# Rounded passes for the late blocks of the value product, a deferred sum, a third turn of scatter tables and shorter scatters

## The reference

```python
q = _rope(einsum('bim,ghmd->bghid', x, w_aq)); k = _rope(einsum('bim,gmd->bgid', x, w_ak))
v = einsum('bim,gmd->bgid', x, w_av)                     # G = 4 groups, H = 4 heads, D = 128
s = einsum('bghid,bgjd->bghij', q * D**-0.25, k * D**-0.25) - 1e30 * (i < j)
o = einsum('bghij,bgjd->bghid', softmax(s), v)           # the value product
x = _layernorm(x + einsum('bghid,ghdm->bim', o, w_ao))   # the out-projection and its sum
# experts: grouped top-6 of 64 by sigmoid scores; of an expert's tokens those with a place below CAP = 48 count
y = segment_sum(topk_w * (silu(buf @ w_gate) * (buf @ w_up)) @ w_down)
out = _layernorm(x + y + (silu(x @ ws_gate) * (x @ ws_up)) @ ws_down)
```

## Time and profile before

| | us |
|---|---|
| median of 3 runs | 1127.45 (1126.43 to 1128.49) |
| the profiled execution | 1126.55, its span 1124.7 |
| PE busy | 1017.0 (90%) |
| DVE busy | 562.6 (50%) |
| ACT busy | 518.7 (46%) |
| POOL busy | 363.4 (32%) |
| mean granted clock of PE | 0.96 |

### The profile page before, as it was taken

How to read it: one execution, slowest core, us unless ns; L and a number is a source line. 1 busy time by engine, 2 the same in 40 slices (tenths; PEclk the granted TensorE clock), 3 DMA queues, 4 the chain that set the end, 5 groups by cost and what they waited for, 6 DMA issues and landing times.

```text
span 1124.7 us, 16829 instructions
## 1 busy us (share of the span) xinstructions
PE 1017.0 (90%) x5312; PEld 731.9 (65%) x5312; DVE 562.6 (50%) x1533; ACT 518.7 (46%) x1147; POOL 363.4 (32%) x402
## 2 busy tenths in 40 slices
PE   6999998789999999999998899999999999657825
PEld 4888887566667776767666666777776676434512
DVE  5766765365554454443425675454535444323306
ACT  3333334454564556454543555464645645133312
POOL 6666665123322212103033313313021121035641
PEclk9999999799999999999999999999999999868868
DMA  7455233533321111111113323333211033968558
GB/s 230 163 180 183 105 117 108 163 91 106 95 63 62 53 56 49 38 43 51 34 44 98 101 80 95 112 104 100 65 39 52 26 92 91 245 178 175 80 100 315
DMA packets 99462, 117.57 MB, mean 105 GB/s; under 512 B 16065, under 2 KB 69173, under 8 KB 99376
## 3 DMA queue, kind: packets, MB, share of 16 engines
q1 hardware_dynamic: 76752, 87.65, 25.3%
q10 hardware_dynamic: 13408, 22.09, 6.5%
q0 software_dynamic: 9216, 6.76, 4.0%
HBM read 76.48 MB, written 53.35 MB: 115 GB/s over the span
## 4 chain that ended last, share of the span: by engine, by line
PE 75%; DMA 9%; DVE 6%; issue 4%; ACT 3%; SPq 2%; POOL 1%; ACTq 0%; POOLq 0%; DVEq 0%
PE o_ps L986 21%; PE s_ps L963 16%; PE ring L973 11%; PE ring L994 10%; DMA sums<-erow,goal_u 6%; PE s_ps L934 6%; PE ring L934 5%; PE s_ps L941 1%; SPq L657 1%; PE s_ps L966 1%; DVE neg_max L1150 1%; ACT probs L820 1%; DMA fsum<-sums 1%; PE o_ps L934 1%; PE ring L941 1%
## 5 line engine op out<-in xcount | busy, mean ns | idle before, releaser
L986 PE MATMUL o_ps<-pt,v 128*128 128x512 f32 x576 | 297.2, 598 | 3.9 <-DVE ot L1165 3.8
L828 ACT ACTIVATE pt<-ring 128x512 f32<-128x512 f32 x288 | 170.9, 594 | 252.1 <-PE ring L973 251.8
L963 PE MATMUL s_ps<-kt,qt_hi 128*128 128x512 f32 (+3 forms) x768 | 261.3, 422 | 3.5 <-issue 1.9
L1150 DVE TENSOR_REDUCE neg_max<-s_ps 128x1 f32<-128x128 f32 (+7 forms) x256 | 191.8, 753 | 135.8 <-PE s_ps L966 135.2
L820 ACT ACTIVATE probs<-s_ps,neg_max 128x128 f32<-128x128 f32 (+7 forms) x256 | 189.3, 740 | 110.2 <-DVE neg_max L1150 102.4
L718 POOL TENSOR_TENSOR qt_lo<-q_raw,qt_hi 128x512 fp32r<-128x512 f32 x64 | 81.2, 1270 | 474.1 <-ACT qt_hi L758 474.1
L963 PEld LDWEIGHTS s_ps<-kt,qt_hi 128*128 128x128 f32 x768 | 139.4, 194 | 79.4 <-issue 61.2
L973 PE MATMUL ring<-ident,probs 128*128 128x128 f32 x1152 | 176.2, 276 | 11.4 <-ACT probs L820 11.3
L973 PEld LDWEIGHTS ring<-ident,probs 128*128 128x128 f32 x1152 | 129.3, 142 | 56.8 <-issue 56.8
L963 PE MATMUL s_ps<-kt,qt_lo 128*128 128x512 f32 (+3 forms) x384 | 134.2, 350 | 0.0
L729 POOL DMA_INDIRECT slot_rows<-row,slot_u x96 | 94.5, 984 | 66.5 <-DVE slot_u L1267 39.7
(11 more groups left out here) (182 smaller groups left out, 1283.7 us busy)
## 6 DMA issues: line engine op xcount, KB each, us to landing
q_rows<-q_out SPq DMA_DIRECT2D x64, 256.0 KB, 2.0
q_raw<-q_rows ACTq DMA_DIRECT2D x64, 256.0 KB, 2.7
inv_row<-inverses SPq DMA_DIRECT2D x64, 256.0 KB, 3.3
fsum<-sums SPq DMA_DIRECT2D x32, 256.0 KB, 6.9
sums<-blank SPq DMA_DIRECT2D x16, 384.0 KB, 2.8
wexp<-in_L_ffn_w_gate_dram SPq DMA_DIRECT2D x32, 192.0 KB, 3.9
wexp<-in_L_ffn_w_up_dram SPq DMA_DIRECT2D x32, 192.0 KB, 4.2
wexp<-in_L_ffn_w_down_dram SPq DMA_DIRECT2D x32, 192.0 KB, 5.0
```

The costliest lines, as they stand in the source:

```text
L828: reader(act.activation(pt[:, n % PTB, :], bank(s), ACT.Copy), s)
L963: pe.matmul(s_ps[:, n % 2, c + a:c + e], q[qp], k[kp][:, a:e], start=(qp == kp == 0), stop=(qp == 1 and not last))
L986: pe.matmul(o_ps[:, :], v_sb[i // NT][:, g, j, :], pt[:, n % PTB, :], start=(j == 0), stop=(j == blocks(u) - 1)).then_inc(pv_done, 1)
L1150: dve.tensor_reduce(neg_max[:, n % 8:n % 8 + 1], s_ps[:, n % 2, score_cols(n)], AX_X, ALU.max, negate=True).then_inc(max_ready, 1)
```

## The change

- For key blocks 3 to 7 (VF = 3) the value product runs as three rounded passes: V and the transposed probabilities are split into a rounded high part (ACT, with the copy it made anyway) and a low part, DVE's subtraction out of PSUM. It is DVE's subtraction that lets the ring bank go. Blocks 0 to 2 stay as they were.
- There is room for one sequence's late V halves only. Those of the second sequence go to memory (v_rows) in the projection and come back group by group as the last tile of the first sequence is done with a group ("vsplit": ACT the high part, POOL the low).
- DVE's and POOL's part of "outproj" becomes a step "yadd", placed at heads (6, 6, 7, 7) where outproj is at (6, 7, 6, 6); norm and all behind it in the later tiles are placed one head later.
- TURNS 3 instead of 2 (6 tables, EB 6), so half as many bytes again to clear and to read back; the scatter-adds take 112 rows (64 + CAP) instead of 128.
- XB, the buffers of x, 2 instead of 3. The value tiles take other places, so that homes come free at other times.

```diff
-EB = 4
-TURNS = 2
+EB = 6
+TURNS = 3
+USED = HALF + CAP
-XB = 3
+XB = 2
+VF = 3
+VS = NT - VF
...
     (("outproj",), -1, (6, 7, 6, 6)),
-    (("norm",), -1, (7, 7, 7, 7)),
-    (("x1t",), -1, (9, 9, 8, 8)),
-    (("rtr",), -1, (11, 11, 9, 9)),
-    (("shared",), -1, (11, 11, 9, 9)),
-    (("pick", 0), -1, (12, 12, 10, 10)),
+    (("yadd",), -1, (6, 6, 7, 7)),
+    (("norm",), -1, (7, 7, 8, 8)),
+    (("x1t",), -1, (9, 9, 9, 9)),
+    (("rtr",), -1, (11, 11, 10, 10)),
+    (("shared",), -1, (11, 11, 10, 10)),
+    (("pick", 0), -1, (12, 12, 11, 11)),
...
             seq.append(("omul", u))
+            if u // G == NT - 1:
+                seq.append(("vsplit", u % G))
...
-        v_sb = [sb("v0", [P, G, NT, D], F32, att)]
+        v_sb = [sb("v0", [P, G, VF, D], F32, att)]
...
+        v = sb("v", [P, G, 2, VS, D], F32R, att)
...
+        pt_hi = sb("pt_hi", [P, PTB, HD], F32R, att)
+        pt_lo = sb("pt_lo", [P, PTB, HD], F32R, att)
...
-                    load_x(s[1] + 2)
+                    load_x(s[1] - 1 + XB)
...
+                if s[0] == "proj" and s[2] == "V" and s[1] >= NT + VF:
+                    j = s[1] - NT - VF
+                    read(sp, s)
+                    sp.dma_start(v_rows[j * P:(j + 1) * P, :], v_out[:, :]).then_inc(v_stored, 16)
+                if s == ("omul", G * (NT - 2)):
+                    sp.wait_ge(v_stored, 16 * VS)
+                    load_v(0)
+                if s[0] == "vsplit" and s[1] + 1 < G:
+                    sp.wait_ge(v_later, s[1] + 1)
+                    load_v(s[1] + 1)
...
-                    load_homes(kt[0], v_sb[0], kt[1], *[v_sb[1][:, 0, :, :]] * (G - 1))
+                    load_homes(kt[0], v_sb[0], kt[1], *[v[:, 0, :, :, :]] * (G - 1))
...
-                if s[0] == "outproj":
+                if s[0] == "vsplit":
+                    g = s[1]
+                    pool.wait_ge(v_later_hi, g + 1)
+                    pool.tensor_tensor(v[:, g, 1, :, :], v_raw[:, :, :], v[:, g, 0, :, :].bitcast(F32), ALU.subtract
+                                       ).then_inc(v_later, 1)
+                if s[0] == "yadd":
                     pool.wait_ge(var_ready, s[1] + 1)
...
-                    sums[:, :], bass.IndirectOffsetOnAxis(ap=goal_u[:, n:n + 1], axis=0),
-                    erow[:, n % EB, :], None, bounds_check=TABLES * TABLE - 1, oob_is_err=True, compute_op=ALU.add
+                    sums[:, :], bass.IndirectOffsetOnAxis(ap=goal_u[0:USED, n:n + 1], axis=0),
+                    erow[0:USED, n % EB, :], None, bounds_check=TABLES * TABLE - 1, oob_is_err=True, compute_op=ALU.add
...
-                    reader(act.activation(pt[:, n % PTB, :], bank(s), ACT.Copy), s)
+                    if s[2] < VF:
+                        reader(act.activation(pt[:, n % PTB, :], bank(s), ACT.Copy), s)
+                    else:
+                        split(pt_hi[:, n % PTB, :], bank(s)).then_inc(p_hi_ready, 1)
...
-                    pe.matmul(o_ps[:, :], v_sb[i // NT][:, g, j, :], pt[:, n % PTB, :],
-                              start=(j == 0), stop=(j == blocks(u) - 1)).then_inc(pv_done, 1)
+                    first, last = j == 0, j == blocks(u) - 1
+                    if j < VF:
+                        ins = pe.matmul(o_ps[:, :], v_sb[i // NT][:, g, j, :], pt[:, n % PTB, :], start=first, stop=last)
+                    else:
+                        for vp, pp in PASSES:
+                            ins = pe.matmul(o_ps[:, :], v[:, g, vp, j - VF, :], (pt_hi, pt_lo)[pp][:, n % PTB, :],
+                                            start=False, stop=(last and vp == 1))
+                    ins.then_inc(pv_done, 1)
...
+                if kind == "ptrans" and s[2] >= VF:
+                    n = PT_AT[s[1:]]
+                    dve.wait_ge(p_hi_ready, PS_AT[s[1:]] + 1)
+                    reader(low(pt_lo[:, n % PTB, :], bank(s), pt_hi[:, n % PTB, :]), s)
...
-                if kind == "outproj":
-                    i = s[1]
+                if kind == "yadd":
+                    i, s = s[1], ("outproj", s[1])
                     dve.wait_ge(attn_ready, i + 1)
```

More of the change, by code:

```diff
@@ L81 @@
     (("outproj",), -1, (6, 7, 6, 6)),
[L82 to L93 removed]
+    (("yadd",), -1, (6, 6, 7, 7)),
[4 more added lines that the diff above has]
+    (("pick", 0), -1, (12, 12, 11, 11)),
+    (("ht",), -1, (13, 13, 12, 12)),
+    (("pick", 1), -1, (13, 13, 12, 13)),
+    (("sd",), -1, (15, 15, 13, 13)),
+    (("pick", 2), -1, (14, 14, 13, 13)),
+    (("pick", 3), -1, (14, 14, 14, 14)),
+    (("pick", 4), -1, (14, 14, 14, 14)),
+    (("pick", 5), -1, (15, 15, 15, 15)),
 ]
@@ L178, in schedule @@
     drain(UNITS)
-    seq += [(s, p) for s in ("outproj", "norm", "x1t", "rtr")] + [("pick", p, n) for n in range(8)]
+    seq += [(s, p) for s in ("outproj", "yadd", "norm", "x1t", "rtr")] + [("pick", p, n) for n in range(8)]
     seq += [(s, p) for s in ("count", "place", "shared", "ht", "sd")]
@@ L222 @@
 PT_ALL = len(PT_AT)
+PS_AT = {k: n for n, k in enumerate(k for k in PT_AT if k[1] >= VF)}
 PROJ_ALL = 6 * TILES
@@ L288, in build @@
         q_out = sb("q_out", [P, QB, HD], F32, pre)
+        v_out = sb("v_out", [P, HD], F32, pre)
         pre.close()
         probs = sb("probs", [P, 2, H, T], F32, att)
-        pt = sb("pt", [P, PTB, HD], F32, att)
+        whole = ExitStack()
+        pt = sb("pt", [P, PTB, HD], F32, whole)
+        whole.close()
+        pt_hi = sb("pt_hi", [P, PTB, HD], F32R, att)
+        pt_lo = sb("pt_lo", [P, PTB, HD], F32R, att)
         ot = sb("ot", [P, G, HD], F32, att)
@@ L310, in build @@
         ahead = sb("ahead", [P, E], F32, att)
-        rest = sb("rest", [P, 96], F32, att)
+        v_sb.append(sb("v1", [P, G, VF, D], F32, att))
+        v_raw = sb("v_raw", [P, VS, D], F32, att)
         q_raw = sb("q_raw", [P, QB, HD], F32, att)
@@ L398, in build @@
         q_ready = sem("q_ready")
+        v_hi_ready = sem("v_hi_ready")
+        v_stored = sem("v_stored")
+        v_loaded = sem("v_loaded")
+        v_later_hi = sem("v_later_hi")
+        v_later = sem("v_later")
+        p_hi_ready = sem("p_hi_ready")
         scores_ready = sem("scores_ready")
@@ L550, in _, with load_v @@
                          ).then_inc(bias_loaded, 16)
-            load_x(1)
-            load_x(2)
+            for n in range(1, XB):
+                load_x(n)
             sp.wait_ge(const_ready, 1)
+            def load_v(g):
+                sp.dma_start(v_raw[:, :, :], v_rows[:, g * D:(g + 1) * D].rearrange("(n p) d -> p n d", p=P)
+                             ).then_inc(v_loaded, 16)
             def load_pair(n):
@@ L653, in _ @@
             for n in range(TURNS):
-                sp.wait_ge(erow_sent[n], 16 * (PAIRS // TURNS))
+                sp.wait_ge(erow_sent[n], 16 * len(range(n, PAIRS, TURNS)))
             for c in range(FINAL):
@@ L783, in _ @@
                     b, j = divmod(s[1], NT)
-                    reader(act.activation(v_sb[b][:, :, j, :], bank(s).rearrange("p (g d) -> p g d", g=G), ACT.Copy), s)
+                    rows = bank(s).rearrange("p (g d) -> p g d", g=G)
+                    if j < VF:
+                        reader(act.activation(v_sb[b][:, :, j, :], rows, ACT.Copy), s)
+                    elif b == 0:
+                        split(v[:, :, 0, j - VF, :], rows).then_inc(v_hi_ready, 1)
+                    else:
+                        used(act, v_stored, 16 * (j - VF))
+                        reader(act.activation(v_out[:, :], bank(s), ACT.Copy), s)
+                if kind == "vsplit":
+                    g = s[1]
+                    act.wait_ge(v_loaded, 16 * (g + 1))
+                    act.wait_ge(pv_done, PT_AT[((NT - 1) * G + g, NT - 1)] + 1)
+                    split(v[:, g, 0, :, :], v_raw[:, :, :]).then_inc(v_later_hi, 1)
                 if kind == "qkt":
@@ L979, in _ @@
                     read(pe, ("ptrans", u, j))
-                    if g == 0 and j == blocks(u) - 1:
+                    if g == 0 and j == blocks(u) - 1 and (i < NT or j < VF):
                         read(pe, ("proj", i, "V"))
+                    if j == VF and i == NT + VF:
+                        pe.wait_ge(v_later, g + 1)
                     if j == 0 and u >= 1:
@@ L1139, in _ @@
                                              wide(sin_sb[:, i % NT, :], 2 * H), ALU.mult), s)
+                if kind == "proj" and s[2] == "V" and VF <= s[1] < NT:
+                    j = s[1] - VF
+                    dve.wait_ge(v_hi_ready, j + 1)
+                    reader(low(v[:, :, 1, j, :], bank(s).rearrange("p (g d) -> p g d", g=G), v[:, :, 0, j, :]), s)
                 if kind == "qkt" and s[2] == "K":
```

24 lines of the change are left out of this document (10 added, 14 removed).

## The result

The changed kernel took 1110.69 us (median of four runs, 1108.96 to 1111.61) beside 1127.97 (1126.43 to 1130.4) of the kernel before on the same chip: a ratio of 0.9852 (95% interval 0.9832 to 0.9873). That is 17.3 us by the medians and 16.7 by the ratio; what follows says of whole kernels how much faster they are by the ratio. The forecast was 1113.0 in a range of 1101 to 1125. The profiled executions have spans of 1124.7 and 1107.1.

What follows compares the result with a forecast made beforehand. PE was taken to bound the attention, the scatters' turns the expert stage, DMA bytes the reading back. Attention -10.9, junction +1, experts -17 and reading back +12.4 sum to -14.5 from 1127.45: 1113.0 us, range 1101 to 1125.

Steps and rivals of the forecast that it cites:

- Value product: Attention, PE: three rounded passes save 0.16 us on each of 120 products from the fourth key block on, -19.3 us.
- What DVE gets: Attention: PE's waits for DVE's 120 new subtractions out of PSUM, 0.69 us each, cost +1.5 us (0 to 10).
- Only heads with two late blocks have the loop ... slack 1.4: Fat tiles: DVE's 3.74 us loop against PE's 3.73 binds only such heads; the low part has 1.4 us to spare.
- rival (c): DVE paces the fat tiles: 32 heads past their slack by 0.8 us lose 26 us, 1139; 0.10 together with another rival.
- The later sum: Out-projection's sum one head later: ring bank held longer in six tiles, +3.5 us; late exp in two second tiles, +2.4.
- The bank stall: Six fat tiles: PE waits 0.5 to 0.75 us for the ring bank the out-projection holds until the later sum.
- Values over memory: Stores, reloads and splits of values: last split in the short tile +0.5, late store +0.5, together +1 us.
- The junction: Between attention and experts: 0.8 MB more weights and zeros queued, mostly hidden behind the router's chain, +1 us (0 to 3).
- The expert stage: Three turns: 20 scatters at 2.1 us, 12 at 1.86, the last 3.8; 68 us against 85, -17 us (-8 to -24).
- The reading back: Last stretch: 48 loads instead of 32, 10.8 us more at 388 GB/s, plus two adds 1.6; +12.4 us (10 to 15).
- Rival (a): DMA engines cap the experts at 2.33 us a scatter all through; the stage gives 8 us, 1122 in all; chance 0.14.
- Rival (b): Everything overlaps: DVE's slack holds, bank free in time, experts near POOL's pace; attention -17, experts -24, 1100 us; chance 0.18.

Runs made afterwards that it cites:

- experiment 6: Changed kernel without DVE's 120 subtractions: all three passes take the probabilities' high half, so PE's work is the same; 1101.6 us, ratio 0.9763.
- 3: Changed kernel with the sum beside the out-projection again and norm to pick placed as in the kernel before; 1115.45 us, ratio 0.9888.
- Experiment 9: Changed kernel with a head's exp behind both copies on ACT instead of between them; 1102.96 us, ratio 0.9787.
- 4: Kernel before with only the order changed: sum one head later, norm to pick placed as in the changed kernel; 1123.15 us, ratio 0.996.
- 7: Changed kernel with reloads and splits of the second sequence's values moved into that sequence's second and third tile; 1108.63 us, ratio 0.9832.
- 11: Changed kernel with exp behind both copies, values' reload two tiles later, last count one head later, eight reading-back loads early; 1100.31 us, ratio 0.9761.
- 5: Changed kernel with its scatters of 128 rows again instead of 112; 1116.89 us, ratio 0.9897.
- experiments 9 to 11: Changed kernel with exp behind both copies (1102.96 us); plus values' reload and last count later (1104.34); plus eight reading-back loads early (1100.31).

## Why the prediction was right

The time (1110.7 for 1113.0) came out, and stage by stage the sum did too: attention -10.1 from first to last out-projection for -10.9, junction +2.4 for +1, scatters -19.7 for -17, reading back +11.6 for +12.4, and 1.8 us ahead of the first out-projection for which there is no term. But within the attention two terms were wrong by 8 and 9 us, and cancelled: that the attention came out is luck.

- **Value product, -19.3: right.** A rounded product is 0.161 to 0.166 us shorter in experiment 6, where nothing else limits PE, against 0.16. The estimate from the Trainium skill, "TensorE: Matmul & The Clock Gate", section "Back-to-back issue gap" (216 ns for an isolated pass), would have meant 0.21. The section says itself that a stream with a weight load for each pass keeps another pace, and gives about 131 ns for it; the 0.233 of this stream agrees with neither.
- **What DVE gets, +1.5 (0 to 10): mis-sized, 10.7 measured** (6 against the changed kernel), just beyond the upper bound. The range held the time all the same only because the next term was wrong the other way. The step that failed is "Only heads with two late blocks have the loop ... slack 1.4". The loop was right to 0.04 us (3.78 for 3.74), and so was the view that six blocks pay nearly nothing (0.17). What I left out is that a loop as long as PE's period has nothing to win back a delay with: the router's clumps that I had named push it (0.9 us at 920.0 to 920.9), and the lag is not won back within the group of heads that have the loop. I had listed just this as rival (c) and priced it at 26 us with 32 heads; it came in two tiles only, and in the last of them the router's place counts too: with the router a head earlier it has no wait for pt_lo (3). Experiment 9 shows the mechanism: the same work without the loop costs 3.2. The 14 us of DVE work that I set beside "31 busy of 67" were misread too: that row is the tile with seven blocks and 16 products, not 20.
- **The later sum, +3.5 and +2.4: wrong in sign, -2.5 measured in the kernel before** (4), and -1.0 in the changed kernel, where the last tile loses 2.25 by it (3). So this term and the one above are not independent. "Putting the sum off gains nothing there" looked at DVE's next reduction alone. The gain seems to come not from the sum, but from the router that moved with it, past the scaling of ot, and lies in tiles with three and four blocks, whose waits I didn't read. The bank stall shows as one wait of 0.2 in each eight-block tile (the ring's for y_sb above). PE's wait for exp in the second tile did come, 1.5 for the 1.2 forecast, and took the place of its waits for row (0.4) and at the router's matmuls (0.6); the interval is the same to 0.01.
- **Values over memory, +1: too little.** The split that falls into the short tile costs 0.9 us where the loop doesn't bind (what is left of experiment 6's intervals after 19.3 and 2.5; 9 and 11, at the same granted clock, differ by 1.0 in the pair) and up to 2.9 in the changed kernel (7), some 0.7 of it by the granted clock. I had counted its 1.56 us on POOL and not that it stands ahead of the power that norm and router wait for.
- **The junction, +1 (0 to 3): open, not contradicted.** +2.4 in these two traces, but four kernels with two turns have 41.4 to 43.1 (mean 42.2) and ten with three turns 42.1 to 44.4 (mean 43.3). The means differ by 1.2, within the scatter of either. The scatter goes with the granted clock of the stretch: the seven kernels with 0.67 or 0.68 have 41.4 to 42.9, the seven with 0.64 or 0.65 have 43.1 to 44.4. Among the first, three turns cost 0.6 us more than two in the mean, among the second 0.8. Which comes first, the longer wait or the lower clock, is not shown.
- **The expert stage, -17: near.** 19.7 us from first to last scatter. The first twenty came 2.11 us apart, as forecast (2.1), and the others 1.76 instead of 1.86: POOL issues 112 rows in 1.45 and not 1.54 us. From one 128-row duration I had taken the issue time to be fixed; rows save 3.6 us of the stage in all (5). And the sum took 32 distances where 32 scatters have 31, 1.9 us too many. What the Trainium skill says in "DMA: Bandwidth & Descriptors", section "Issuing engines are not separate DMA queues", fits: at a share of 0.88 the first part runs slower than POOL could go, and there the 16 rows cost 0.13 us a scatter and not 0.09.
- **The reading back, +12.4: right.** 11.6 in these traces, 12.4 with the tables alone. SP issues 48 loads in 26.8 us where it issued 32 in 16; between 1070 and 1100 the DMA share is 1.00 at 370 GB/s, so that pace follows from the bytes and not from SP.

Rival (a), DMA as the cap at 2.33 us a scatter, fell (2.11, then 1.76). Rival (b), everything overlaps, asked for -17 in the attention: experiments 9 to 11 show that this was to be had by an order (-17.4 from first to last out-projection in 9, 1103 us).

What stays open: why the granted clock falls after the same wait in three kernels and not in a fourth, and the 2.6 us that the last tile still loses in 9 against 6, of which the waits show 1.5 for the choice and 0.6 for pt_lo.

## What to carry to other kernels

When an edit gives a half idle engine a step that stands inside a loop over several engines (reduce, exp, copy, subtract, reduce), compare the loop's length with the bound engine's period, not the volume: at equality every small clump becomes a stall, and a change of order that opens the loop may be worth more than the step costs. Price each move of a step in the tiles where it will pass something, short ones too, and by all that moves with it. And a total that comes out is no proof of its terms: two errors of 8 us with opposite signs were found here only by undoing one part at a time and by comparing intervals that repeat to 0.06 us where the granted clock is the same; put the clock beside every interval before reading a difference of a microsecond.

## Of the hardware

- A scatter-add's issue on POOL depends on its rows: 1.54 us for 128, 1.45 for 112, with 0.30 between.
- Eight loads of 256 KB, sent out while the last scatters were in flight, doubled the time until the last two had landed (7.5 us from the last one's start for 3.6), though they read other tables (window of the trace around it: DMA share 0.89). That their bytes wait with the loads' for the same engines is likely, and not tested by itself.
- PE, DVE and ACT repeat a stage of 50 us to 0.03 us from kernel to kernel (the fifth tile's interval is 50.58 to 50.61 in the ten kernels with rounded passes), as long as the granted clock is the same. After one and the same wait of PE of 2.1 us the clock fell to 0.50 in three kernels and stayed at 1.00 in one, which is 1.15 us.
- The start of the first out-projection differs by 4.9 us between kernels, the junction by 3.0.
